# Edge network of a graph net: first layer summed in PSUM, one-hots of both kinds by VectorE, destinations loaded as rows, four places for table rows

## What is computed

```python
e = jnp.concatenate([h[src], h[dst]], axis=-1)
e = jax.nn.relu(e @ Wm1 + bm1) @ Wm2 + bm2
e = e * drop_mask
m = jax.ops.segment_sum(e, dst, num_segments=n)
z = jnp.concatenate([h, m], axis=-1)
h_new = jax.nn.relu(z @ Wu1 + bu1) @ Wu2 + bu2
```

## Time and profile before

| | |
|---|---|
| median of 3 runs | 11821.93 us (11821.28 to 11841.86) |
| profiled execution | 11807.61 us, its span 11805.9 us |
| TensorE busy | 8012.9 us, 68% |
| GpSimd busy | 7458.2 us, 63% |
| VectorE busy | 2603.4 us, 22% |
| ScalarE busy | 1341.9 us, 11% |
| mean granted TensorE clock | 0.823 of full speed |
| edge network, first gather to last accumulation | 9486.8 us to 11615.2 us |

### The profile page before, as it was taken

How to read it: one execution, slowest core, us unless ns; L and a number is a source line. 1 busy time by engine, 2 the same in 40 slices (tenths; PEclk the granted TensorE clock), 3 DMA queues, 4 the chain that set the end, 5 groups by cost and what they waited for, 6 DMA issues and landing times.

```text
span 11805.9 us, 167099 instructions
## 1 busy us (share of the span) xinstructions
PE 8012.9 (68%) x57412; PEld 6882.2 (58%) x57412; DVE 2603.4 (22%) x4842; ACT 1341.9 (11%) x2812; POOL 7458.2 (63%) x7263
## 2 busy tenths in 40 slices
PE   0133334333688876888688878887888678788877
PEld 0133333332566765667567667776667567777775
DVE  2322222222211123111311121112111323333331
ACT  0100000000210012000200020002000322222221
POOL 1555555555377755777477757775777267777772
PEclk9766666666789987999799979997999588888887
DMA  8222222222144433444344434443444233333332
GB/s 301 76 67 65 70 64 67 65 70 64 50 110 114 113 93 100 113 113 114 104 113 113 112 87 114 113 113 86 114 114 112 68 77 77 76 77 78 77 76 58
DMA packets 620843, 1119.43 MB, mean 95 GB/s; under 512 B 238297, under 2 KB 240651, under 8 KB 620785
## 3 DMA queue, kind: packets, MB, share of 16 engines
q1 hardware_dynamic: 358194, 703.96, 20.9%
q0 software_dynamic: 229792, 332.84, 12.7%
q10 hardware_dynamic: 32800, 81.92, 1.7%
HBM read 978.01 MB, written 140.12 MB: 95 GB/s over the span
## 4 chain that ended last, share of the span: by engine, by line
POOL 34%; PE 24%; issue 23%; DMA 12%; ACT 3%; DVE 2%; SPq 2%; ACTq 0%; POOLq 0%; DVEq 0%
POOL G L525 32%; PE PS L1594 11%; PE PS L1515 8%; DMA G<-table,IDX 5%; DMA amat<-SVAL,SIDX 3%; DMA xres<-work 2%; PE PS L1469 2%; POOL amat L549 2%; SPq L335 1%; PE PS L1603 1%; ACT work L692 1%; PE PS L1537 1%; PE PS L1433 0%; ACT IDX L766 0%; PE PS L1448 0%
## 5 line engine op out<-in xcount | busy, mean ns | idle before, releaser
L525 POOL DMA_INDIRECT G<-table,IDX x6272 | 6364.7, 1015 | 2054.8 <-issue 1971.9
L1594 PE MATMUL PS<-PARTS,work 125*128 125x288 bf16 (+1 forms) x30000 | 3879.5, 289 | 88.2 <-DMA work<-amat 88.2
L1594 PEld LDWEIGHTS PS<-PARTS,work 125*128 125x128 fp8e4 x30000 | 2956.7, 99 | 905.1 <-issue 89.8
L1515 PE MATMUL PS<-work,G 128*96 128x128 f32 (+1 forms) x9408 | 1528.6, 331 | 2619.0 <-DMA G<-table,IDX 2051.0
L1515 PEld LDWEIGHTS PS<-work,G 128*96 128x96 f32 (+1 forms) x9408 | 1400.2, 207 | 2753.1 <-DMA G<-table,IDX 1984.4
L1172 DVE TENSOR_TENSOR AGG<-AGG,PS 96x128 f32 (+1 forms) x784 | 221.7, 283 | 6074.2 <-PE PS L1515 5997.3
L549 POOL DMA_INDIRECT amat<-SVAL,SIDX x784 | 773.4, 987 | 937.6 <-ACT IDX L766 609.6
L1167 DVE TENSOR_TENSOR work<-IOF,REL 128x1024 f32<-128x1024 f32 x784 | 952.4, 1215 | 69.8 <-SPq L384 26.7
L1238 DVE TENSOR_SCALAR_CACHE_REDUCE work<-work,KEYC 128x384 bf16<-128x384 f32 x784 | 479.5, 612 | 623.4 <-DMA work<-keys 510.3
L766 ACT ACTIVATE IDX<-SRC 128x8 int32 (+1 forms) x784 | 160.9, 206 | 3825.9 <-PE PS L1515 3825.7
L1469 PE MATMUL PS<-W,work 97*125 97x96 f32 (+1 forms) x1800 | 388.3, 412 | 266.9 <-ACT work L692 127.3
(11 more groups left out here) (184 smaller groups left out, 4079.7 us busy)
## 6 DMA issues: line engine op xcount, KB each, us to landing
work<-amat SPq DMA_DIRECT2D x1500, 320.0 KB, 2.9
G<-table,IDX POOLq DMA_INDIRECT x6272
amat<-work ACTq DMA_DIRECT2D x50, 1600.0 KB, 18.3
work<-in_edge_attr_dram SPq DMA_DIRECT2D x196, 384.0 KB
work<-keys SPq DMA_DIRECT2D x98, 640.0 KB, 6.4
table<-work SPq DMA_DIRECT2D x70, 468.8 KB
xres<-work SPq DMA_DIRECT2D x30, 468.8 KB
work<-xres POOLq DMA_DIRECT2D x30, 468.8 KB, 4.4
```

The costliest lines, as they stand in the source:

```text
L525: pool.indirect_dma_start(G[:, k, i, 0:D], None, table, bass.IndirectOffsetOnAxis(ap=IDX[:, k, i:i + 1], axis=0)).then_inc(done, 16)
L1515: last = pe.matmul(PS[0:rows, k, 0:WIN], G[:, k, i, 0:rows], OH[k][:, i, :], start=(i == 0), stop=(i == TPG - 1))
L1594: last = pe.matmul(PS[:, 2, 0:width], AB[m][0:NP, jj * WIN:(jj + 1) * WIN].bitcast(FP8), PARTS[0:NP, j * PW:j * PW + width], start=(j == 0 ...
```

## The change

- The one-hots in turned form (nodes on partitions, edges along the columns) are no longer made by turning `OH` on TensorE and copying on ScalarE. SyncE loads the group's 1024 destinations as one row, broadcast to 128 partitions (`destinations`, into `DROW`, two places), and VectorE compares it with the node that each partition stands for (`turned`; `PLACE` holds base plus partition for each group and is made once in the setup). `OHT` has two places. The comparison reads `DROW` with a step of 8 elements, since edge p*8+i belongs to column i, and waits for the first layer of the group before (`e_pre`).
- The hidden layer's sum is made in PSUM with the features on the partitions (`first_layer`): per half a group one matmul of `QW` with 512 columns of `OHT`, then four matmuls that add the gathered columns of `G` through the identity. `q_to_edges`, `hidden_sum` and `turn_hidden` are gone. `PRE_B` has two pairs of banks.
- The place in `G` is free, and the next indices are written, when `first_layer` is done (`e_pre`); ScalarE does this ahead of relu, and relu now waits for the output layer of the group before (`e_out`).
- `QW` has four places, loaded two groups ahead (`table_window`).
- TensorE's order: first layer of g + 1, output layer of g, sums of g. VectorE's: turned one-hots of g + 2, products of g, accumulation of g, one-hots of g + 2. The loops of SyncE and TensorE run over four groups instead of two.
- `DROW` and `MSG` lie where `XL` (x of the node stages) lies, so GpSimd waits for the last accumulation before the last node stage's loads. SyncE waits for the end of the node stage's splitting (`n_lo`) before its first load.

```diff
-        QW = sb("QW", [P, 2, D])
+        QW = sb("QW", [P, 4, D])
...
-        OHT = work[:, 3584:3584 + GE]
-        MSG = work[:, 4608:4608 + TPG * D].rearrange("p (i f) -> p i f", i=TPG)
-        PRE = work[:, 5376:5376 + TPG * D].rearrange("p (i f) -> p i f", i=TPG)
+        OHT = [work[:, 3584 + k * GE:3584 + (k + 1) * GE] for k in range(2)]
+        DROW = [work[:, 8840 + k * GE:8840 + (k + 1) * GE].bitcast(I32) for k in range(2)]
+        MSG = work[:, 10888:10888 + TPG * D].rearrange("p (i f) -> p i f", i=TPG)
...
+        PLACE = sb("PLACE", [P, GROUPS])
...
+        TURN_B, PRE_B, OUT_B = (0, 4), ((5, 6), (2, 3)), (1, 7)
...
+            def table_window(g, k, reused=True):
+
+                if reused:
+                    sp.wait_ge(e_pre, g * 2 - 6)
+                base = load(sp, ET.SP, BASE_I[0:1, bass.ds(g, 1)], N - 1)
+                sp.dma_start(QW[:, k, :], qtable[bass.ds(base, WIN), :]).then_inc(e_q[k], 16)
...
             def edge_loads(g, row, k):
-
                 sp.wait_ge(e_sum, g + 1)
...
-                base = load(sp, ET.SP, BASE_I[0:1, bass.ds(g, 1)], N - 1)
-                sp.dma_start(ATTR[k], attributes(row)).then_inc(e_attr[k], 16)
-                sp.dma_start(QW[:, k, :], qtable[bass.ds(base, WIN), :]).then_inc(e_q[k], 16)
-
...
+                sp.dma_start(ATTR[k % 2], attributes(row)).then_inc(e_attr[k % 2], 16)
...
+            def destinations(g, row, k, reused=True):
+                if reused:
+                    sp.wait_ge(e_oht, g - 1)
+                sp.dma_start(DROW[k % 2], t["dst"][bass.ds(row, GE)].rearrange("(a e) -> a e", a=1
+                                                                             ).to_broadcast([P, GE])
+                             ).then_inc(e_dst[k % 2], 16)
...
+            sp.wait_ge(n_lo, 2 + 7 * NCH)
+            destinations(0, 0, 0, False)
+            for g in range(2):
+                table_window(g, g, False)
...
+            with sp.Fori(1, GROUPS // 4 - 1) as i:
+                for k in range(4):
+                    g = i * 4 + k
+                    edge_loads(g, g * GE, k)
+                    table_window(g + 2, (k + 2) % 4)
+                    destinations(g + 1, (g + 1) * GE, k + 1)
...
+            pool.wait_ge(e_oht, GROUPS)
+            pool.wait_ge(e_acc, 2 + GROUPS)
+            with pool.If(n_extra > 0):
+                pool.wait_ge(x_acc, 1 + 7 * EXTRA)
...
                 index(1, 1, 2, e_sum, e_idx)
-                copy_turned(1, e_turn, e_oht)
                 with act.Fori(0, GROUPS // 2 - 1) as i:
                     for k in range(2):
                         g = i * 2 + k
-                        relu(g * 2, e_pre, e_rel)
-
-                        index(g + 2, k, g * 2 + 2, e_add, e_idx)
-                        copy_turned(g + 2, e_turn, e_oht)
-                relu(GROUPS * 2 - 4, e_pre, e_rel)
-                copy_turned(GROUPS, e_turn, e_oht)
-                relu(GROUPS * 2 - 2, e_pre, e_rel)
+
+                        index(g + 2, k, g * 2 + 2, e_pre, e_idx)
+                        act.wait_ge(e_out, g * 2 + 2)
+                        relu(g * 2, k, e_pre, e_rel)
+                for g in (GROUPS - 2, GROUPS - 1):
+                    act.wait_ge(e_out, g * 2 + 2)
+                    relu(g * 2, g % 2, e_pre, e_rel)
...
+            link(dve.tensor_scalar(PLACE[:, :], XTAB[:, 2, :], PCOL[:, 0:1], None, ALU.add))
...
-            def hidden_sum(k, v, q2e, done):
+            def messages(k, v, outs, done, first=0):
                 for b in range(2):
-                    dve.wait_ge(q2e, v + (b + 1))
-                    dve.tensor_tensor(PRE[:, 4 * b:4 * b + 4, :],
-                                      PS[:, Q_B[b], 0:4 * D].rearrange("p (i f) -> p i f", f=D),
-                                      G[:, k, 4 * b:4 * b + 4, 0:D], ALU.add).then_inc(done, 1)
-
...
             def edge_network():
-                def hidden(g, k, pair):
-                    dve.wait_ge(e_rows[k], pair * (16 * TPG) + 16 * TPG)
-                    hidden_sum(k, g * 2, e_q2e, e_add)
+                def turned(g, k, pair):
+
+                    dve.wait_ge(e_dst[k], pair * 16 + 16)
+                    dve.wait_ge(e_pre, g * 2)
+                    dve.tensor_scalar(OHT[k].rearrange("w (i p) -> w i p", i=TPG),
+                                      DROW[k].rearrange("w (p i) -> w i p", i=TPG), PLACE[:, bass.ds(g, 1)], None,
+                                      ALU.is_equal).then_inc(e_oht, 1)
 
                 def message(g, k, pair):
                     dve.wait_ge(e_attr[k], pair * 16 + 16)
-                    messages(k, g * 2, e_out, e_msg)
+                    messages(k, g * 2, e_out, e_msg, 2)
...
                 ready(6)
-                make(0, 0, 1, e_sum, e_oh)
-                make(1, 1, 2, e_sum, e_oh)
-                hidden(0, 0, 0)
+                for k in range(2):
+                    turned(k, k, 0)
+                    make(k, k, k + 1, e_sum, e_oh)
                 with dve.Fori(0, GROUPS // 2 - 1) as i:
                     for k in range(2):
                         g = i * 2 + k
+                        turned(g + 2, k, i + 1)
                         message(g, k, i)
-                        hidden(g + 1, 1 - k, i + k)
                         add(g, k, g, e_sum, e_acc, D, net=True)
                         make(g + 2, k, g + 3, e_sum, e_oh)
                 message(GROUPS - 2, 0, GROUPS // 2 - 1)
-                hidden(GROUPS - 1, 1, GROUPS // 2 - 1)
...
-            for s, v in ((a_sum, 2), (e_sum, 2), (f_sum, 2), (d_mm, AC)):
+            for s, v in ((a_sum, 2), (e_sum, 2), (f_sum, 2), (e_out, 2), (d_mm, AC)):
...
-            def q_to_edges(k, done):
-
-                for i in range(TPG):
-                    last = pe.matmul(PS[:, Q_B[i // 4], (i % 4) * D:(i % 4 + 1) * D], OHT[:, i * P:(i + 1) * P],
-                                     QW[:, k, :], start=True, stop=True)
-                    if i % 4 == 3:
-                        last.then_inc(done, 1)
-
-            def turn_hidden(v, added, done):
-                for i in range(TPG):
-                    if i % 4 == 0:
-                        pe.wait_ge(added, v + (i // 4 + 1))
-                    last = pe.transpose(PS[0:D, PRE_B[i // 4], (i % 4) * P:(i % 4 + 1) * P], PRE[:, i, :],
-                                        ident[:, :])
-                    if i % 4 == 3:
-                        last.then_inc(done, 1)
+            def first_layer(k, q, done):
+
+                for b in range(2):
+                    bank = PRE_B[k][b]
+                    pe.matmul(PS[0:D, bank, :], QW[:, q, :], OHT[k][:, b * HE:(b + 1) * HE], start=True, stop=False)
+                    for i in range(4):
+                        last = pe.matmul(PS[0:D, bank, i * P:(i + 1) * P], G[:, k, 4 * b + i, 0:D], ident[:, :],
+                                         start=False, stop=(i == 3))
+                    last.then_inc(done, 1)
...
             def edge_network():
-                def q_part(g, k, pair):
+                def hidden_layer(g, k, quad):
                     pe.wait_ge(e_oht, g + 1)
-                    pe.wait_ge(e_q[k], pair * 16 + 16)
-                    q_to_edges(k, e_q2e)
-
-                def group(g, k, pair, last=False):
-
-                    turn_hidden(g * 2, e_add, e_pre)
-                    if not last:
-                        pe.wait_ge(e_oh, g + 2)
-                        turn_one_hots(1 - k, e_turn)
+                    pe.wait_ge(e_q[k % 4], quad * 16 + (k // 4 + 1) * 16)
+                    pe.wait_ge(e_rows[k % 2], quad * (32 * TPG) + (k // 2 + 1) * 16 * TPG)
+                    first_layer(k % 2, k % 4, e_pre)
+
+                def rest(g, k):
                     pe.wait_ge(e_acc, g + 2)
                     edge_out(g * 2, e_rel, e_out)
-                    if not last:
-                        q_part(g + 1, 1 - k, pair + k)
-                    message_sums(k, g * 2, e_msg, e_sum)
-
-                pe.wait_ge(e_oh, 1)
-                turn_one_hots(0, e_turn)
-                q_part(0, 0, 0)
-                with pe.Fori(0, GROUPS // 2 - 1) as i:
-                    for k in range(2):
-                        group(i * 2 + k, k, i)
-                group(GROUPS - 2, 0, GROUPS // 2 - 1)
-                group(GROUPS - 1, 1, GROUPS // 2 - 1, last=True)
+                    pe.wait_ge(e_oh, g + 1)
+                    message_sums(k % 2, g * 2, e_msg, e_sum)
+
+                hidden_layer(0, 0, 0)
+                with pe.Fori(0, GROUPS // 4 - 1) as i:
+                    for k in range(4):
+                        hidden_layer(i * 4 + k + 1, k + 1, i)
+                        rest(i * 4 + k, k)
```

51 lines of the change are left out of this document (27 added, 24 removed).

## The result

| | before | after |
|---|---|---|
| median of 4 runs | 11821.6 us (11820.37 to 11841.86) | 12096.38 us (12090.72 to 12101.62) |
| profiled execution | 11807.61 us | 12090.72 us, its span 12089.0 us |
| edge network, first gather to end of the last | 9486.8 to 11606.9 us, 10.82 us a group | 9494.7 to 11884.8 us, 12.19 us a group |

The change makes the kernel slower: ratio 1.0228, 95% interval 1.0211 to 1.0246, 275 us. The forecast was slower by 36 us, with a range that ended at 11965 us; direction right, size wrong by a factor of more than seven. Of the 283 us by which the spans differ, 270 lie in the edge network.

A forecast was written before the change was run, and what follows sets the result against it. GpSimd's gathers were taken to bound the kernel. From the profiled 11807.6 us, +35 us of stalls, +1 and +0.4 at the ends gave 11844; with the runs' median 14.3 above, the forecast was 11858 us, range 11780 to 11965.

The forecast's parts named there:

- GpSimd sets the pace, TensorE's work is off the path: Edge network: gathers take 10.05 us a group, 1969 of 2128 us; removed matrix work gives nothing beyond its effect on gathers.
- the bound of 124 us on any gain: Edge network: gathers' prolongation, 0.63 us a group; no more can come back, as the other 1969 us are the gathers.
- Rival 5: TensorE becomes the bound once a group takes over 10.85 us, as at mean clock below 0.7; +176 to +872 us, chance 0.07.
- 8.3 us a group ... under the 10.68 ... Price nothing: Loop of destinations' load, comparison, products and sums: 8.3 us, at most 10.2, under the gathers' 10.68, so priced at nothing.
- the other path (15.3 us a group): TensorE's whole group at half clock, 15.3 us, considered for a backlog that delays G's release; the average group 9.0 us.
- VectorE's wait for the destinations ending on a DMA, with TensorE idle behind it: Edge network: listed among the signs that would show the forecast wrong; no size or chance given.
- TensorE's sums wait for them, no gather does: Edge network: a late destinations load delays VectorE's work and TensorE's sums but holds up no gather, so it costs nothing.
- The stall formula: VectorE comparison of length D holds gathers D squared over 2T, T = 1.257 us: one-hot 0.585, new 0.22 us a group.
- Rival 3: The new comparison stalls no gather, its 8-element stride or integer input making it slow, 1.3 us; about 11812 us, chance 0.20.
- nothing (as line 1238): Lower bound on the new comparison's stall: line 1238's counting, a scalar comparison, let a gather beside it finish in 0.97 us.
- G comes free later, at nothing: Index writes wait for the new matmuls, 5.7 us, at half clock 9.5, covered by the other buffer's 10.05 us of gathers.
- The ends: After the last gather the output matmuls start 1 us later, at half clock 5; one more setup comparison adds 0.4 us.

The follow-up runs named there:

- e7: e1 with the one-hot's counters and the comparison's place operand in PSUM, so neither comparison has a second SBUF operand or the scalar form: 11711.83 us, ratio 0.9915.
- e6: The kernel before, with the edge network's one-hots reading their row of counters from PSUM: 11693.62 us against 11806.68, ratio 0.9904.
- e1: The changed kernel, with SyncE loading the destinations of group g + 2 ahead of the attributes of g: 11938.47 us against 11811.11, ratio 1.0113.
- e4: The kernel before plus one comparison of the new form per group, into a spare buffer that nothing reads: 11979.01 us against 11811.11, ratio 1.0143.
- e5: e1 with the comparison reading at step 1 instead of 8, so other values are computed: 11792.83 us (one run) against 11806.68.

## Why the prediction was right in sign and wrong in size

**GpSimd sets the pace, TensorE's work is off the path: right.** e7 against e6 shows the redistribution of matrix work as worth nothing; the bound of 124 us on any gain was met by e6's 113. The 3.73 us that the prediction gave the new first layer at full clock are 3.70 in the trace after (10515.58 to 10519.28 us). Rival 5, TensorE as the bound, looked at the wrong condition: TensorE's total stayed under the period (1798 us busy of 2380, clock 0.80), and its clock hurt through a loop instead.

**"8.3 us a group ... under the 10.68 ... Price nothing": this is the step that failed,** worth 136 us. The loop was seen and written down in the right order, but it came out at 8.3 us where 12.45 was measured, 1.43 us of it short in issuing and landing and most of the rest in the sums:

| term | predicted | after |
|---|---|---|
| issuing behind attributes and table rows, landing | 5.5 us | 1.52 + 5.41 us |
| comparison to products | 0.75 us | 1.06 us |
| products to sums | 2 x 0.56 us | 0.70 us |
| sums to the next load | 0.95 us (half of them, full clock) | 3.60 + 0.16 us (all, low clock) |
| sum | 8.3 us, upper bound 10.2 | 12.45 us |

Most of this could be read before. The sums run in two halves, and each waits for one product; so the first half runs beside the second product, and what stands in the loop is one product and all of the sums, 0.56 + 1.91 = 2.47 us, not 1.12 + 0.95 = 2.07. Landing had an upper bound of 6.4 + 1 us, and 6.93 was measured, inside it. At that bound the loop is 7.4 + 0.75 + 2.47 = 10.6 us at full clock: level with 10.68, with nothing to spare. What carried it over is the clock: with the sums at the low level, 2 x 1.91 = 3.82 us, the same terms make 12.5 us, and 12.45 was measured. That sums double at half clock stood in my own text for the other path (15.3 us a group) and was not applied here. The text also named the sign, "VectorE's wait for the destinations ending on a DMA, with TensorE idle behind it", which is what the rows of L1346 and L1569 now show; it had no case among the rivals and no chance. "TensorE's sums wait for them, no gather does" was wrong by one step: the next first layer stands behind the sums on TensorE, and the indices wait for it.

**The stall formula met the size in e1, partly by luck; the length put into it was wrong.** With D = 1.165 us, D squared over 2T is 0.54 us a group; e1 has 106 us / 196 = 0.54. It is not a law: in e4 the same comparison holds gathers for 143 us where the formula gives 104, in e5 for 30 where it gives 46, and the one-hot, 115 by the formula, takes 125 in the kernel before, 136 in e1 and 52 in e5. The phase decides, as the prediction warned. Nor is the comparison's hold the one that the formula describes, that of the one-hot: it reaches gathers that started up to some 0.45 us ahead of it too, and in e1 194 of 196 comparisons hold one. The predicted D of 0.75 came from rows with unit step, where the comparison reads with a step of 8: 0.22 us became 0.54, and the one-hot beside it lies worse as well (136 us against 125). Term by term: predicted +35 us, measured +116 in e1 and +66 in the changed kernel, where gathers that wait for indices meet VectorE less often. e5 gives 767 ns, so 0.75 was right for step 1.

**Rival 3 was half right:** the step does put the comparison near the slow pace (1.15 us, not 1.3), yet it holds gathers. The earlier trace rows had suggested the opposite, with a gather that kept its time; but that counting ends at 601.09 us, and a gather held until 0.12 us behind it would be over at 601.21, while it ended at 601.40 anyway: the row could not have shown a hold. Other gathers of the same stage can. One that starts within the comparison is held until 0.83 us after its end; beside the counting of line 1238 this one ends 0.55 us after:

```profile
519.64 0.61 DVE L1238 TENSOR_SCALAR_CACHE_REDUCE work<-work,KEYC 128x384 bf16<-128x384 f32 x1 [0.18 <-DVE work L1238]
519.83 0.97 POOL L525 DMA_INDIRECT G<-table,IDX  x1 [0.30 <-issue]
```

In the kernel before, 39 gathers start 0.15 to 0.45 us into such a counting with no one-hot beside them, and none takes over 0.98 us; in e1, 33 start so into the new comparison, and none takes under 1.53 us. So the bound "nothing (as line 1238)" was true of the counting, which also sums, and did not carry over to the plain form. The holding goes with the form and its operands, not with the pace: e7's 2005 ns with a PSUM operand holds none.

**"G comes free later, at nothing": right** as soon as the loop is gone, 12.5 us of index waits in e1. **The ends:** last gather to the end of the span 199.0 us before, 204.2 after; +5 us, the half-clock figure of the prediction.

**The rule from the Trainium skill,** SBUF — State Buffer, section "SBUF: two separate sides", spoke against the change, and it bears out: both the two-input form and the plain scalar form hold gathers, and e6 shows that one operand in PSUM frees them. That sentence would have been worth more as a question to the kernel before, where 124 us lay open, than as a cost of the change.

## What to carry to other kernels

A load that is issued behind the last step of one group and needed by the same step of the next is a loop: add its terms at their upper bounds, with TensorE at its low clock, before pricing it at nothing, since the idle time that it makes can itself lower the clock. Where GpSimd issues gathers at the pace that binds, look for VectorE instructions with two SBUF operands or in the plain scalar form beside it: putting one small constant operand into PSUM cost nothing and gave 1.0% here. Price a strided elementwise instruction from a row with that stride, and a hold from a row of the same instruction: the counting that spared the gathers was another form.
